# The scan stage of a four-layer kernel: prologue in separate banks, shared units moved, front work ahead of a wait

## The reference

```
xc, z = split(x @ W_in.T)                 # 512 + 512 channels
xc = silu(causal_conv(xc, W_conv, 4 taps))
dlt, B, C = split(xc @ W_xproj.T)         # 16, 16, 16
delta = softplus(dlt @ W_dt.T + b_dt)
h_t = exp(delta * -exp(A_log)) * h_{t-1} + delta * B * xc
y_t = sum_n C_t,n h_t,n + D * xc
out = (y * silu(z)) @ W_out.T             # W_out is applied in the next stage
```

## Time and profile before

| | |
|---|---|
| median of 3 runs | 5016.26 us (5009.55 to 5017.32) |
| profiled execution | 5021.53 us, span 5019.7 us |
| mean granted PE clock | 0.938 |
| busy over the span | PE 4311.7 us (86%), DVE 3481.3 (69%), ACT 2808.3 (56%), POOL 1880.3 (37%) |
| scan stage | 0 to about 1017 us of the span |

### The profile page before, as it was taken

The page is one execution under the profiler, slowest core; times in us unless marked ns, Lnnn a source line. Parts: engine busy times, 40 slices in busy tenths (PEclk is TensorE's granted clock), DMA queues, the critical chain, the costliest instruction groups (busy, mean ns, idle before and its releaser), DMA issues. The chain is left out here.

```text
span 5019.7 us, 82035 instructions
## 1 busy us (share of the span) xinstructions
PE 4311.7 (86%) x19960; PEld 3024.2 (60%) x19991; DVE 3481.3 (69%) x7239; ACT 2808.3 (56%) x6575; POOL 1880.3 (37%) x1548
## 2 busy tenths in 40 slices
PE   7888888789998979999999999999866549999970
PEld 2333333346665558888888888888755437777750
DVE  6999999944443878888888888888744433333338
ACT  6777777522221058888888888888733224444430
POOL 6888888701000021212122121212145543333337
PEclk8999999999999989999999999999977769999985
DMA  1000000021102531212211120212144335545558
GB/s 43 13 13 13 13 13 9 9 95 43 41 14 93 178 96 27 52 25 54 52 31 50 26 59 25 52 26 56 47 144 145 132 120 155 156 152 155 156 169 299
DMA packets 308603, 382.80 MB, mean 76 GB/s; under 512 B 123410, under 2 KB 238994, under 8 KB 302372
## 3 DMA queue, kind: packets, MB, share of 16 engines
q1 hardware_dynamic: 235428, 262.85, 17.4%
q0 software_dynamic: 26112, 73.44, 4.2%
q10 hardware_dynamic: 46944, 45.16, 3.3%
HBM read 228.20 MB, written 153.11 MB: 76 GB/s over the span
## 5 line engine op out<-in xcount | busy, mean ns | idle before, releaser
L1653 DVE TENSOR_TENSOR probsT<-ps_t,probsT 128x512 fp32r<-128x512 f32 (+3 forms) x1280 | 779.7, 609 | 137.4 <-ACT probsT L1593 116.6
L1593 ACT ACTIVATE probsT<-ps_t 128x512 fp32r<-128x512 f32 (+3 forms) x1280 | 685.5, 536 | 258.4 <-PE ps_t L1441 234.4
L1585 ACT ACTIVATE probs<-ps_s,negm 128x512 f32<-128x512 f32 (+3 forms) x1297 | 811.4, 626 | 28.1 <-DVE negm L1646 27.2
L1453 PE MATMUL ps_o<-probsT,vbuf 128*128 128x512 f32 (+3 forms) x2560 | 815.9, 402 | 6.8 <-ACT folding L1599 6.2
L1428 PE MATMUL ps_s<-kbuf,qbuf 128*128 (+1 forms) x2602 | 768.8, 380 | 59.1 <-ACT probs L1585 31.3
L1633 DVE TENSOR_REDUCE pmax<-ps_s 128x1 f32<-128x512 f32 (+3 forms) x1301 | 778.0, 601 | 48.9 <-PE ps_s L1428 24.8
L1441 PE MATMUL ps_t<-idn,probs 128*128 128x128 f32 x4352 | 696.3, 275 | 13.9 <-DVE probsT L1653 13.9
L472 POOL TENSOR_TENSOR dBx<-u,b_all 128x1024 f32<-128x1024 f32 x256 | 610.2, 2393 | 107.4 <-DVE h L571 92.6
L1441 PEld LDWEIGHTS ps_t<-idn,probs 128*128 128x128 f32 x4352 | 518.1, 142 | 134.9 <-DVE probsT L1653 41.0
L1536 POOL CAST qbuf<-qstage 128x512 fp32r<-128x512 f32 x132 | 81.0, 614 | 1273.6 <-DMA qstage<-q_scr 762.8
L248 PE MATMUL ps_y<-hc,idn 128*128 128x512 f32 x1024 | 513.8, 625 | 49.2 <-POOL hc L479 47.7
(11 more groups left out here) (258 smaller groups left out, 7008.8 us busy)
## 6 DMA issues: line engine op xcount, KB each, us to landing
xr<-xs ACTq DMA_DIRECT2D x294, 136.0 KB
parts<-y SPq DMA_DIRECT2D x36, 1024.0 KB, 5.0
qstage<-q_scr SPq DMA_DIRECT2D x528, 64.0 KB
w_gu<-W_guT SPq DMA_DIRECT2D x64, 384.0 KB
q_scr<-rot SPq DMA_DIRECT2D x64, 256.0 KB, 2.9
attn<-ostage SPq DMA_DIRECT2D x128, 128.0 KB
at<-attn SPq DMA_DIRECT2D x32, 512.0 KB
w_d<-W_downT SPq DMA_DIRECT2D x64, 192.0 KB
```

What stands on the lines that cost most here:

```text
L1453: last = nc.tensor.matmul(ps_o[:, lo:], vbuf[:, kb, :, :], probsT[:, g % SLOTS, part, lo:], start=kb == 0 and part == 0, stop=kb == BAND * ...
L1585: nc.scalar.activation(probs[:, k, at:at + n, :], ps_s[:, u % RING, 0:n * P], ACT.Exp, bias=negm[:, tile, :], accum_out=sums[:, s, j, c:c ...
L1593: nc.scalar.activation(probsT[:, g % SLOTS, 0, lo:], ps_t[:, t % 2, lo:], ACT.Copy).then_inc(high_t.sem, 1)
L1653: nc.vector.tensor_tensor(probsT[:, g % SLOTS, 1, lo:], ps_t[:, t % 2, lo:], probsT[:, g % SLOTS, 0, lo:].bitcast(F32), ALU.subtract).then ...
```

## The change

- **Places.** GpSimd weighs units 0, 18, 20 and 22 of each chunk instead of 18, 20, 25 and 27. The SiLU of z's second half moves from place 22 to 16, behind the second SiLU of xc, with one exp table load behind both.
- **PE's order.** In a shared unit the front work of the next unit is issued between `spread_c` and the wait for GpSimd's `hc`. The `skip` matmuls stand ahead of `sum_states` of their unit instead of behind it.
- **Prologue.** `in_proj` of blocks 1 to 3 goes to the banks of `ps_a`, `x_proj` and two of the four `dt_proj` to `ps_y`, so PE waits for fewer evacuations. The second `dt_proj` is issued before the first spreads. ACT casts the selection, between its first two SiLUs. ACT does `take_b` after softplus of its half. DVE makes the first `u` and the first `dBx` instead of GpSimd.

```diff
-    SILU_X_AT, SILU_Z1_AT, SILU_Z0_AT = (14, 16), 22, 1
+    SILU_X0_AT, SILU_Z1_AT, SILU_Z0_AT = 14, 16, 1
     SOFT_AT, DELTA_AT = (24, 28), (27, 31)
     U1_AT, U0_AT = 2, 29
-    SHARED_AT = (18, 20, 25, 27)
+    SHARED_AT = (0, 18, 20, 22)
...
+        def bank(kind, k, j=0):
+
+            if k == 0 and kind == "x" and j:
+                return ps_a[:, j - 1, :]
+            if k == 0 and kind == "xp":
+                return ps_y[:, 0, :]
+            if k == 0 and kind == "dt" and j % 2 == 0:
+                return ps_y[:, 1, :]
+            return ps_f[:, :]
...
+            def in_proj(use, k, part, to=None):
+                if to is None:
+                    freed(use)
                 for kd in range(KD):
-                    last = nc.tensor.matmul(ps_f[:, :], w_in[:, kd, part * P:(part + 1) * P], xt[:, k % 2, kd, :],
+                    last = nc.tensor.matmul(ps_f[:, :] if to is None else to, w_in[:, kd, part * P:(part + 1) * P], xt[:, k % 2, kd, :],
                                             start=kd == 0, stop=kd == KD - 1)
                 last.then_inc(front_ps.sem, 1)
...
-                if hv == 0:
+                if hv == 0 and k:
...
-                freed(use_of("dt", k, d))
-                nc.tensor.matmul(ps_f[:, :], w_dt[:, d * P:(d + 1) * P], dt_in[:, :],
+                freed(use_of("dt", k, d) - int(k == 0 and d > 0))
+                nc.tensor.matmul(bank("dt", k, d), w_dt[:, d * P:(d + 1) * P], dt_in[:, :],
...
+            def skip_input(q):
+                c, hv, _ = parts_of(q)
+                for i in range(DH):
+                    d = hv * DH + i
+                    nc.tensor.matmul(ps_y[:, i, :], skip[:, d, :], xc[:, c % 2, d, :], start=False, stop=False)
+
+            def front(q):
...
+                in_proj(use_of("x", 0, j), 0, j, bank("x", 0, j))
+            pe.wait_ge(zeroed.sem, 2)
+            pe.wait_ge(consts.sem, 16 * CONSTS)
+            for hv in range(HALVES):
+                x_proj(0, hv)
+            dt_proj(0, 0)
+            for d in range(DB):
+                if d + 1 < DB:
+                    dt_proj(0, d + 1)
+                if d == 0:
+                    pe.wait_ge(sel_ready.sem, 2)
+                    spread_c(0)
+                spread_b(0, d)
+            for j in range(DH):
+                in_proj(use_of("z0", 0, j), 0, DB + j)
+            pe.wait_ge(skip_ready.sem, DB)
+            for q in range(UNITS):
+                if not (q and shared(q - 1)):
+                    front(q)
                 if shared(q):
                     pe.wait_ge(c_taken.sem, shared_no[q])
                 else:
                     pe.wait_ge(hc_done.sem, q + 1 - shared_no[q])
                 if q + 1 < UNITS:
                     spread_c(q + 1)
+                if q % STEPS in SKIP_AT:
+                    skip_input(q)
                 if shared(q):
+                    front(q + 1)
                     pe.wait_ge(hc_shared.sem, shared_no[q])
                 sum_states(q)
...
-            for hv in range(HALVES):
-                act.wait_ge(tap_done.sem, (hv + 1) * DH * TAPS)
-                silu_x(0, hv)
+            act.wait_ge(tap_done.sem, DH * TAPS)
+            silu_x(0, 0)
+            act.wait_ge(consts.sem, 16 * CONSTS)
+            for part in range(2):
+                half = slice(part * NST, (part + 1) * NST)
+                nc.scalar.activation(sel[:, half, :], sel_in[:, half, :], ACT.Copy).then_inc(sel_ready.sem, 1)
+            act.wait_ge(tap_done.sem, DB * TAPS)
+            silu_x(0, 1)
             exp_tables()
-            act.wait_ge(consts.sem, 16 * CONSTS)
             nc.scalar.activation(neg_a[:, :, :], a_log[:, :, :], ACT.Exp).then_inc(nega_step.sem, 1)
             act.wait_ge(nega_step.sem, 1)
             nc.scalar.activation(neg_a[:, :, :], neg_a[:, :, :], ACT.Copy, scale=-1.0).then_inc(nega_step.sem, 1)
@@ -407,9 +434,10 @@
             for hv in range(HALVES):
                 for d in range(hv * DH, (hv + 1) * DH):
                     evac_dt(0, d)
-                    take_b(0, d)
                 for part in range(3):
                     softplus(0, hv, part)
+                for n in range(hv * DH, (hv + 1) * DH):
+                    take_b(0, n)
                 if hv == 0:
                     for s in range(RING):
                         decay(s)
@@ -446,6 +474,8 @@
                     silu_z(c, 0)
                     exp_tables()
                 if v == SILU_Z1_AT:
+                    if k < CHUNKS:
+                        silu_x(k, 1)
                     silu_z(c, 1)
...
-                pool.wait_ge(reduce_done.sem, reduce_done.at(q - 2))
+                if q >= 2:
+                    pool.wait_ge(reduce_done.sem, reduce_done.at(q - 2))
...
-            pool.wait_ge(consts.sem, 16 * CONSTS)
-            for part in range(2):
-                half = slice(part * NST, (part + 1) * NST)
-                nc.gpsimd.tensor_copy(sel[:, half, :], sel_in[:, half, :]).then_inc(sel_ready.sem, 1)
             halo(0)
-            make_u(0, 0)
-            drive(0)
+            pool.wait_ge(first_drive.sem, 1)
+            pool.sem_inc(dbx_done.sem)
             drive(1)
...
+            dve.wait_ge(delta_ready.sem, delta_ready.at(0, 1))
+            dve.wait_ge(xc_ready.sem, xc_ready.at(0, 1))
+            nc.vector.tensor_tensor(u[:, 0:DH, :], delta[:, 0, 0:DH, :], xc[:, 0, 0:DH, :], ALU.mult).then_inc(u_ready.sem, 1)
+            dve.wait_ge(u_ready.sem, u_ready.at(0, 1))
+            dve.wait_ge(b_taken.sem, b_taken.at(0, 1))
+            nc.vector.tensor_tensor(dBx[:, 0, :, :], u[:, 0:DH, :], b_all[:, 0:1, :].to_broadcast((P, DH, TC)),
+                                    ALU.mult).then_inc(first_drive.sem, 1)
+            dve.wait_ge(first_drive.sem, 1)
```

More of the change, by code:

```diff
@@ L137, in mamba @@
         u_ready = tally("u_ready", HALVES)
+        first_drive = tally("first_drive")
         b_ready = tally("b_ready", NST)
@@ L294, in _ @@
                         in_proj(use_of("z0", k, j), k, DB + j)
+            pe.wait_ge(front_ld.sem, 32)
+            pe.wait_ge(xt_ld[0].sem, 16)
+            for j in range(DB):
+                in_proj(use_of("x", 0, j), 0, j, bank("x", 0, j))
[17 more added lines that the diff above has]
+                    front(q)
                 if shared(q):
@@ L313, in evac_x @@
                     act.wait_ge(halo_done.sem, halo_done.at(k - 1))
-                nc.scalar.activation(xraw[:, j, TAPS - 1:], ps_f[:, :], ACT.Copy).then_inc(front_ev.sem, 1)
+                nc.scalar.activation(xraw[:, j, TAPS - 1:], bank("x", k, j), ACT.Copy).then_inc(front_ev.sem, 1)
             def evac_xp(k):
                 act.wait_ge(front_ps.sem, use_of("xp", k) + 1)
-                nc.scalar.activation(dt_in[:, :], ps_f[0:RANK, :], ACT.Copy)
-                nc.scalar.activation(dbc[:, k % 2, :], ps_f[0:PARTS, :], ACT.Copy).then_inc(high_done.sem, 1)
+                nc.scalar.activation(dt_in[:, :], bank("xp", k)[0:RANK, :], ACT.Copy)
+                nc.scalar.activation(dbc[:, k % 2, :], bank("xp", k)[0:PARTS, :], ACT.Copy).then_inc(high_done.sem, 1)
             def evac_dt(k, d):
                 act.wait_ge(front_ps.sem, use_of("dt", k, d) + 1)
-                nc.scalar.activation(delta[:, k % 2, d, :], ps_f[:, :], ACT.Identity,
+                nc.scalar.activation(delta[:, k % 2, d, :], bank("dt", k, d), ACT.Identity,
                                      bias=dt_bias[:, d:d + 1]).then_inc(front_ev.sem, 1)
@@ L455, in _ @@
                             tap(k, i // 2, 2 * (i % 2) + t)
-                    if v in SILU_X_AT:
-                        silu_x(k, SILU_X_AT.index(v))
+                    if v == SILU_X0_AT:
+                        silu_x(k, 0)
                         exp_tables()
```

7 lines of the change are left out of this document (2 added, 5 removed).

## The result

The changed kernel takes 4990.3 us (median of 5 runs, 4988.2 to 4993.7) against 5016.3 (5009.6 to 5024.9): ratio 0.9946, 95% interval 0.9933 to 0.9958, so 21 to 34 us less. The profiled execution has a span of 4987.5 us against 5019.7; the last gate of the scan stage starts at 984.76 instead of 1016.65, which is 31.9 of the 32.2 us. The later stages moved as a block.

The account below looks back on a forecast made before the run. DVE bounds the scan stage, with 28.4 us of `ps_c` waits to win. 13.6 + 12.8 - 0.4 - 1.0 - 1.0 - 3.1 = 20.9, with prologue 22.4: 5021.53 to 4999.1, less 5.3 for the median, forecast 4994 us (4984 to 5010).

Parts of the forecast that it names:

- Cause, the clock after PE's stand at 20: Shared unit 20: PE stands 2.78 us for `hc`, then a 3.78 us sum and `dt_proj` delay the spread DVE awaits.
- I take the fall, and the wait at 22, as gone: Chunks 0, 1, 3, 4: front work ahead of the `hc` wait ends the clock fall and place-22 waits, 13.6 us won.
- The charge of 3.1 us for one fall: Shared units 20 and 22: one fall of PE's clock in seven chunks was allowed for, costing 3.1 us.
- Places 25 and 27 free, 12.8 us: Units 25 and 27 weighed on DVE again: waits at places 26 and 28 to 31 go, 6.2 + 6.6 us.
- The 1.0 us for the other chunks: New shared unit 22, chunks other than 0 and 4: 0.2 us charged for each, 1.0 us together.
- Place 0 for nothing: Sharing place 0, where DVE has the gate and GpSimd is idle: costs nothing, with 0.5 us of cover.
- the freed time at 22 is worth nothing: ACT at place 22: moving one SiLU to 16 gains nothing there, as ACT was not waited for.
- Prologue, +1.5 (-0.5 to +3.5): Prologue up to scan 4: 2.8 to 4.6 us won, 1.1 to 3.3 given back, net taken as 1.5 us.
- given back: Prologue: `take_b` and z projections behind softplus delay the fourth decay and scan 4, returning 1.1 to 3.3 us.
- the first rival: Stands at 20 and 22 still lower PE's clock, each of seven chunks losing about 3.1 us: 5008 us, 15%.
- the slow rival: New waits at places 0 and 22 both lower PE's clock, 3.1 us at each of 16 places: 5036 us, 5%.
- The rival of the prologue: z in_proj runs warm, under 1 us given back, prologue +4.5 us, and no clock fall at all: 4986 us, 15%.

Follow-up runs that it names:

- e4: Kernel before plus two matmuls whose result nobody reads, filling PE's stand at place 20, order of `dt_proj` unchanged: 5005.3 us median, ratio 0.9982.
- e1: Kernel before with only the next unit's front work moved ahead of PE's wait for GpSimd's `hc`: 5003.5 us median, ratio 0.9978.
- e5: Changed kernel with GpSimd weighing unit 27 instead of 22 in each chunk: ratio 0.9958 to the kernel before, steady piece 926.1 us.
- e2: Kernel before with only the shared units moved to 0, 18, 20 and 22: ratio 0.9995, steady piece 947.7 us against 947.8.
- e9: Changed kernel with the z SiLU back at place 22: 4991.9 us, ratio 0.9957 to the kernel before, steady piece 927.6 us.
- f1: Changed kernel with a fifth shared unit, 24, weighed by GpSimd: steady piece 935.8 us against 920.6, one run.
- e6: Changed kernel with the cast of the selection back on GpSimd: scan 4 starts at 68.6 us, steady piece 920.5 us, one run.
- e8: Changed kernel with `take_b` behind each evacuation, ahead of softplus, as before: scan 4 starts at 66.3 us, steady piece 920.4 us, one run.
- e7: Changed kernel with the first `u` and first drive back on GpSimd: scan 4 starts at 65.7 us, steady piece 919.9 us, one run.
- e3: Kernel before with only the second half's z SiLU moved from place 22 to 16: ratio 0.9993 (0.9984 to 1.0003), steady piece 940.8 us.

## Why the prediction was right, point by point

Forecast 4994 (own range 4986 to 5003, range 4984 to 5010), measured 4990.3; gain forecast 22.4 us, measured 27 by the ratio. In the steady piece the forecast was 20.9 and the trace has 27.2. The difference: the waits that I left in (7.5 us) were only 3.5, which is 4.0 us; other waits 1.7 and `make_delta` 4.1, which I had not counted; and against them 1.1 for a weighing and 2.3 of short gaps, which I had not counted either. So the mechanism was right in its largest term, and the closeness of the total owes something to errors of both signs.

- *Bound by DVE, and the 28.4 us of `ps_c` as what can be won:* right; 26.2 us came out of it. I expected 7 us to be left, and 2.2 were.
- *Cause, the clock after PE's stand at 20:* right, shown by e4. Over the sum behind that stand the granted clock of the kernel before was 0.50 in chunks 0, 1, 3 and 7 (3.78 us), 0.64 in chunk 4 (2.98 us) and 1.00 in chunks 2, 5 and 6 (1.98 to 1.99 us). What I said of the remedy was right in size and wrong in one step: "I take the fall, and the wait at 22, as gone". The stand shrank to 1.6 to 1.7 us as worked out, but the sum behind it still ran at the low clock in three of seven chunks (3.2 to 3.6 us). What took the waits away is that `dt_proj` no longer stands behind the sum (e1) and that DVE wants `ps_c` for 23 only, as 22 is shared (2.3 us, e5). The charge of 3.1 us for one fall was too high: the three falls cost 0.74 us together.
- *Places 25 and 27 free, 12.8 us:* right, in e2 as in the changed kernel. That the new unit 22 costs 0.5 us in chunks 0 and 4: 0.55 us in chunk 0; in chunk 4 the wait for a late `ps_c` (0.74) came ahead of it. The 1.0 us for the other chunks was not needed. The stand at 22 was 1.7 us in chunks 0, 1, 3 and 6, not 1.1, and under 0.3 where the sum of 20 had run slowly.
- *Chunk 7:* 2.1 us expected at place 23, 2.2 measured at 24, of which 0.75 for `hc` and 1.46 for `ps_c`.
- *Place 0 for nothing:* right in the changed kernel, where no DVE wait lies there. With PE's old order it does cost something (e2).
- *SiLUs: "the freed time at 22 is worth nothing":* wrong. It was judged against the kernel before, in which 22 isn't shared. With 22 shared, `take_c` and `evac_dt` stand ahead of the SiLU block on ACT, and it is worth 7.0 us (e9); e2 showed the same waits. The sum was still right, since it had charged nothing for leaving it at 22. The step that failed is that each edit was priced alone. On the steady piece the places alone won 0.1 us (e2), PE's order alone 14.1 (e1), and all but the SiLU's place 20.2 (e9).
- *Missing from the sum:* `make_delta` without GpSimd's work beside it, 4.1 us (5.3 the other way round in e5).
- *Prologue, +1.5 (-0.5 to +3.5):* too low for the profiled pair, 4.7; over all traces with either prologue 1.9 to 4.7. `low_parts` ended at 31.75, between the 33.0 and the 31.2 that I gave. From there (T) `make_delta` started at T+6.05 for T+6.2 and the first scan at T+9.9 for T+10.0; that close only because the clock was high at first (first `dt_proj` 1.12 us), for in e5 and f1 (2.07 us) the same code had T+7.85 and T+11.7. The step that failed is "given back": scan 1's second half started at T+20.2, not T+21.4, as the first z projection started at T+15.4, not T+16.3; the second one ran at the high clock in 1.98 us; and scan 4 started at T+32.4, below my T+34.2 to T+36.4 (T+34.2 in e5 and f1). Of the parts the cast is worth 2.8 us (e6), the order of `take_b` 0.6 to 2.4 by the draw of the clock (e8), the first drive on DVE nothing (e7); separate banks by themselves were not tried.
- *Rivals:* the clock did fall all the same, as the first rival had it, but at nearly no price; the slow rival did not occur (no stand on GpSimd at place 0 that a DVE wait followed). The rival of the prologue (it keeps what it wins, +4.5) was the nearer one in the profiled pair.

Left open: what e3 is worth alone; the `skip` matmuls ahead of the sum, which no run tried by themselves; what decides PE's clock behind a stand and in the prologue; and 2.3 us of short gaps ahead of the weighings.

## What to carry to other kernels

When TensorE stands waiting for another engine's result, the wait can be paid twice, as here: once as time and once as a lower clock for what stands behind it (in the kernel before 2.78 us of stand, and a sum of 3.78 us at a granted clock of 0.50 instead of 1.99 us at 1.00). Look at what lies between the end of that stand and the next thing that the bounding engine wants, and move out of it whatever does not need the result. Price edits of one schedule together: places that are free in the old order can be full in the new one, as ACT's place 22 was, and the trace of before cannot show that unless it is walked through in the new order for every engine. And work that fills a gap on GpSimd can cost more on DVE than it takes off it, without any wait being shown (f1: 18.1 us for 9.8): check the duration of the DVE operations that run beside it. Last, when the total's spread is as large as the edit, measure between two fixed instructions of the stage that was touched, and look at the same code in several traces before a difference of 1 or 2 us is given to an edit.
